# Latent attention on one core: head-by-head scaling on GpSimd, and more of the block transfers issued there

## The reference

```python
q = einsum('bld,dhk->blhk', xn, Wq)          # 16 heads of 64
latent = einsum('bld,dc->blc', xn, Wkv_down) # 64 numbers per token
k = einsum('blc,chk->blhk', latent, Wk_up)
v = einsum('blc,chk->blhk', latent, Wv_up)
attn = softmax(where(causal, q @ k / sqrt(64), -inf))   # per head, over keys
s = einsum('bqhd,hdo->bqo', attn @ v, Wout)
```

## Time and profile before

| | us |
|---|---|
| median of three runs | 2358.87 |
| profiled execution, time | 2362.68 |
| its span, first to last instruction | 2360.9 |
| PE busy | 2083.6 (88%) |
| DVE busy | 1713.2 (73%) |
| POOL busy | 1501.1 (64%) |
| ACT busy | 1314.0 (56%) |
| 1400 to 2360 us: PE, DVE, POOL busy | 834.56, 732.20, 724.99 |
| the same stretch, granted clock, DMA share | 0.92, 0.70 |

### The profile page before, as it was taken

One profiled execution on the slowest core, in us unless ns is written; L12 is line 12 of the kernel. 1 busy time (PEld: TensorE's weight loads), 2 busy tenths in 40 slices (PEclk: granted clock), 3 DMA queues, 4 the chain that ended last, 5 costly groups with the idle time before them and its releaser, 6 DMA issues. The chain is left out here.

```text
span 2360.9 us, 45085 instructions
## 1 busy us (share of the span) xinstructions
PE 2083.6 (88%) x15232; PEld 1619.0 (69%) x15232; DVE 1713.2 (73%) x3132; ACT 1314.0 (56%) x3178; POOL 1501.1 (64%) x1337
## 2 busy tenths in 40 slices
PE   6579999999899899999998678889998988898885
PEld 4467777777777777777777566667676767676764
DVE  5587776777767887777674277787788778877783
ACT  3346666766576567666674264545554565455541
POOL 2475666656655666566663147786778777877874
PEclk8789999999999999999999889999998999999988
DMA  8343333333333433333322127676767676767675
GB/s 278 96 104 78 91 93 90 81 90 86 91 79 98 112 88 77 83 88 92 85 66 72 73 75 167 183 180 160 185 179 184 164 188 172 186 167 182 167 178 142
DMA packets 190049, 298.19 MB, mean 126 GB/s; under 512 B 52264, under 2 KB 97660, under 8 KB 188796
## 3 DMA queue, kind: packets, MB, share of 16 engines
q1 hardware_dynamic: 172924, 257.53, 42.8%
q10 hardware_dynamic: 12288, 24.13, 4.2%
q0 software_dynamic: 4608, 13.64, 2.3%
HBM read 56.04 MB, written 20.97 MB: 33 GB/s over the span
## 5 line engine op out<-in xcount | busy, mean ns | idle before, releaser
L1750 PE MATMUL ps<-g_turned,g_latV 128*64 128x256 f32 (+1 forms) x1984 | 306.9, 456 | 47.9 <-issue 22.9
L2032 POOL TENSOR_TENSOR g_pt<-g_pt,g_rl 128x1024 f32<-128x1024 f32 (+2 forms) x112 | 293.8, 2628 | 62.5 <-DVE g_rl L1966 58.3
L854 ACT ACTIVATE l_pp<-ps,l_mx 128x256 f32<-128x256 f32 (+1 forms) x512 | 228.8, 464 | 162.9 <-DVE l_mx L991 162.9
L2032 POOL TENSOR_TENSOR g_pp<-g_pp,g_rl 128x768 f32<-128x768 f32 (+3 forms) x112 | 239.2, 2142 | 74.2 <-DVE g_rl L1966 73.4
L1130 POOL TENSOR_TENSOR l_pp<-l_pp,l_rl 128x1024 f32<-128x1024 f32 (+1 forms) x128 | 229.7, 1795 | 83.5 <-DVE l_rl L999 83.5
L1854 ACT ACTIVATE g_pp<-ps,g_mx 128x128 f32<-128x128 f32 (+3 forms) x256 | 173.5, 688 | 180.1 <-DVE g_mx L1948 78.0
L1854 ACT ACTIVATE g_pt<-ps,g_mx 128x256 f32<-128x256 f32 (+3 forms) x256 | 201.3, 798 | 122.4 <-DVE g_mx L1948 73.1
L1750 PEld LDWEIGHTS ps<-g_turned,g_latV 128*64 128x64 f32 x1984 | 149.5, 149 | 144.5 <-issue 88.9
L1147 POOL TENSOR_TENSOR l_act_lo<-l_u,l_act_hi 114x512 fp32r<-114x512 f32 x96 | 125.6, 1308 | 163.9 <-ACT l_act_hi L904 163.7
L1980 DVE STREAM_TRANSPOSE g_bt<-g_pt 128x1024 f32<-128x1024 f32 (+1 forms) x176 | 194.9, 1129 | 31.3 <-issue 12.6
L991 DVE CUSTOM_DVE_ANT_0 ps<-ps,l_mask 128x256 f32<-128x256 f32 (+1 forms) x512 | 188.4, 441 | 8.0 <-PE ps L703 8.0
(11 more groups left out here) (200 smaller groups left out, 6206.5 us busy)
## 6 DMA issues: line engine op xcount, KB each, us to landing
l_pt<-l_bt SPq DMA_DIRECT2D x1024, 64.0 KB, 2.0
g_turned<-g_bt SPq DMA_DIRECT2D x288, 128.0 KB, 3.4
g_turned<-g_bt SPq DMA_DIRECT2D x288, 96.0 KB, 2.5
g_turned<-g_bt SPq DMA_DIRECT2D x192, 112.0 KB, 3.0
g_turned<-g_bt SPq DMA_DIRECT2D x192, 80.0 KB, 2.4
l_tab<-turns SPq DMA_DIRECT2D x64, 128.0 KB, 2.1
g_turned<-g_bt ACTq DMA_DIRECT2D x64, 128.0 KB, 4.1
g_turned<-g_bt SPq DMA_DIRECT2D x96, 64.0 KB, 2.0
```

What stands on the lines that cost most here:

```text
L854: act.activation(PP[:, i % NP, at, 0:n], ps[:, bank + a, jj * 2 * P:jj * 2 * P + n], ACT.Exp, bias=mx[:, g % 2, h, at:at + 1], scale=-1.0, ...
L1750: last = pe.matmul(o, latV[:, b % 2, c, :], turned[:, :, a, c, :, :], start=(c == 0), stop=(c == t), skip_group_check=True)
L2032: pool.tensor_tensor(view, view, rl[:, u % 2, mine(k):mine(k) + n].unsqueeze(2).to_broadcast([P, n, keys(u)]), ALU.mult).then_inc(s["scale ...
```

## The change

Three things are changed at once.

First, for tiles 4 to 7 the scaling is done head by head. Each of the two heads of a step gets a TENSOR_SCALAR whose factor is one number per partition, in place of one TENSOR_TENSOR over both. `scaled` counts heads and no longer steps, so that the transpose of the first head waits for that head alone. Short tiles keep their instruction.

Second, the transfers are shared out anew:

| units | SP | ACT | POOL |
|---|---|---|---|
| short, before | 12 | 4 | 0 |
| short, now | 11 | 2 | 3 |
| long, before | 12 | 2 | 2 |
| long, now | 10 | 2 | 4 |

Third, the planner's numbers are others (COST, all of RANK, the cost of the two events), so the order on all engines is another one.

```diff
-    ASIDE = (((0, 0), (1, 1), (2, 2), (3, 3)),) * LONG + (((0, 0), (1, 1)),) * (NT - LONG)
-    BELOW = ((),) * LONG + (((2, 2), (3, 3)),) * (NT - LONG)
-    COST = (5.066, 3.78, 2.794, 2.559, 4.043, 4.94, 3.575, 3.892)
+    ASIDE = (((0, 0), (1, 1)),) * LONG + (((0, 0), (1, 1)),) * (NT - LONG)
+    BELOW = (((2, 2), (3, 3), (0, 1)),) * LONG + (((2, 2), (3, 3), (0, 1), (1, 2)),) * (NT - LONG)
+    COST = (4.133, 3.956, 2.412, 2.415, 6.582, 4.423, 1.923, 5.704)
...
-        "pool": {"split_x": -32.9, "scale": -8.81, "divide": 18.37, "move": -1.14},
-        "sp": {"xn": 13.3, "f": -27.73, "x": 55.61, "move": -13.19, "store": 61.01},
+        "pool": {"split_x": -63.04, "scale": -18.63, "divide": 15.72, "move": 0.58},
+        "sp": {"xn": -29.07, "f": 6.53, "x": 30.67, "move": -13.51, "store": 15.24},
...
-            return {"share": 0.12, "exp": 0.235 + 0.00084 * w, "scale": 0.06 + 0.00183 * w * heads}.get(
+            return {"share": 0.12, "exp": 0.235 + 0.00084 * w,
+                    "scale": 0.12 + 0.001 * w if self.long(n) else 0.06 + 0.00183 * w * heads}.get(
...
-            return {"act": 0.635 * aside, "pool": 1.0 * below, "sp": 0.635 * (16 - aside - below)}[engine]
+            return {"act": 0.65 * aside, "pool": 0.53 * below, "sp": 0.635 * (16 - aside - below)}[engine]
...
-                        dve.wait_ge(s["scaled"], first[u - 1])
+                        dve.wait_ge(s["scaled"], heads[first[u - 1]])
...
-                    dve.wait_ge(s["scaled"], k + 1)
+                    dve.wait_ge(s["scaled"], heads[k] + a + n)
...
-                def scale(k):
+                def scale(k, a):
 
                     u, p = pairs[k]
                     pool.wait_ge(s["rl"], k + 1)
-                    n = plan.wide(units[u][1])
+                    n, at = plan.wide(units[u][1]), mine(k, a)
+                    if plan.long(k):
+                        pool.tensor_scalar(probs(k, a), probs(k, a), rl[:, u % 2, at:at + 1], None, ALU.mult
+                                           ).then_inc(s["scaled"], 1)
+                        return
                     view = probs(k, 0, n).rearrange("p (a n) -> p a n", a=n)
                     pool.tensor_tensor(view, view, rl[:, u % 2, mine(k):mine(k) + n].unsqueeze(2).to_broadcast([P, n, keys(u)]),
-                                       ALU.mult).then_inc(s["scaled"], 1)
+                                       ALU.mult).then_inc(s["scaled"], n)
```

More of the change, by code:

```diff
@@ L1180 @@
     LONG = NT // 2
-    ASIDE = (((0, 0), (1, 1), (2, 2), (3, 3)),) * LONG + (((0, 0), (1, 1)),) * (NT - LONG)
-    BELOW = ((),) * LONG + (((2, 2), (3, 3)),) * (NT - LONG)
-    COST = (5.066, 3.78, 2.794, 2.559, 4.043, 4.94, 3.575, 3.892)
+    ASIDE = (((0, 0), (1, 1)),) * LONG + (((0, 0), (1, 1)),) * (NT - LONG)
+    BELOW = (((2, 2), (3, 3), (0, 1)),) * LONG + (((2, 2), (3, 3), (0, 1), (1, 2)),) * (NT - LONG)
+    COST = (4.133, 3.956, 2.412, 2.415, 6.582, 4.423, 1.923, 5.704)
     RANK = {
[L1185 to L1190, removed]
-        "pool": {"split_x": -32.9, "scale": -8.81, "divide": 18.37, "move": -1.14},
-        "sp": {"xn": 13.3, "f": -27.73, "x": 55.61, "move": -13.19, "store": 61.01},
+        "pe": {"latent": -46.39, "values": -18.27, "query": -40.4, "scores": -24.34, "weigh": 9.36, "wout": 40.96,
+              "back": 23.84},
+        "act": {"split_x": 36.71, "latent": -40.62, "values": -46.6, "query": -41.22, "exp": -15.61, "evacuate": -5.65,
+              "gate": -13.09, "move": -3.02},
+        "dve": {"latent": -25.14, "query": -44.88, "largest": 9.59, "share": 2.47, "blocks": 23.4, "gate": 12.45,
+              "back": 36.84},
+        "pool": {"split_x": -63.04, "scale": -18.63, "divide": 15.72, "move": 0.58},
+        "sp": {"xn": -29.07, "f": 6.53, "x": 30.67, "move": -13.51, "store": 15.24},
     }
@@ L1226, in __init__ @@
         events = {"scores": [e for k in range(K) for e in self.steps(k)], "share": [("share", k) for k in range(K)],
-                  "exp": [("exp", k, a) for k, a in heads], "scale": [("scale", k) for k in range(K)],
+                  "exp": [("exp", k, a) for k, a in heads], "scale": [("scale", k, a) for k, a in some],
                   "largest": [("largest", k, a) for k, a in apart], "blocks": [("blocks", k, a) for k, a in some],
@@ L1337, in needs @@
             elif kind == "share":
-                out += [("act", end(n))] + ([("pool", ("scale", last))] if lead else [])
+                out += [("act", end(n))] + ([("pool", tail("scale", last))] if lead else [])
             elif kind == "scale":
@@ L1341, in needs @@
             else:
-                out += [("pool", ("scale", n))]
+                out += [("pool", ("scale", n, event[2]))]
                 if lead and event[2] == 0:
@@ L2064, in _ @@
                     elif e[0] == "scale":
-                        scale(e[1])
+                        scale(e[1], e[2])
                     elif e[0] == "divide":
```

## The result

| | time | ratio to before, 95% interval |
|---|---|---|
| before | 2358.33 us | |
| changed | 2566.32 us | 1.0876 [1.084, 1.0913] |

The change makes the launch 208 us slower. I had forecast 2330, and 2368 as the upper end. The profiled execution has a span of 2563.1 us. First the page's chain of the changed kernel, then its windows (columns as in the earlier trace rows; the stage now runs from 1356 to 2560 us).

A forecast was written before the change was run, and what follows sets the result against it. SP's queue issuing block transfers, 23.6% of the chain, was taken as the bound, PE close behind. Terms -34 -6 +4 +1 = -35 us, cut by 6 to -29 for PE, gave 2330 us against the median; range 2298 to 2368.

The forecast's parts named there:

- The scaling: Long tiles on POOL: 256 one-head instructions priced like a CAST, 230 us in place of 379.5, 150 less.
- dear end: Long tiles' scaling on POOL if TENSOR_SCALAR runs as TENSOR_TENSOR does: 1.67 ns per element, 404 us, 25 more.
- Its worth: Cheaper scaling's effect on time: half of DVE's 11.8 us of waits for POOL credited, 6 us; ends 0 and 12.
- SP's issues: SP's queue: 160 fewer issues, 115 us, of which 29% on the path: 34 us gained; bounds 0 and 115.
- POOL's queue: 224 more issues on POOL at 520 ns, 116 us, queue 691 us in all; cost taken 4 us, bounds 0 and 23.
- the landing: Transfers issued from POOL land later than from SP (128 KB: 4.0 against 3.4 us); cost taken 1 us.
- rival B: PE and DVE take up SP's slack at once; time within 6 us either way, say 2355; chance 0.22.
- 20 as a sign of being wrong: Forecast wrong if DVE's waits for POOL's scaling or PE's for transfers grow by more than 20 us.
- The order: New ranks on all engines: taken as 0, with some 20 us possible either way.
- D: POOL becomes the late queue, with scaling at the dear end, from about 1.5 ns an element; 2374 us; chance 0.12.
- C: More than the sum: waits vanish on both sides, PE runs closer and its clock rises; 2306 to 2295; chance 0.14.
- over 1.3 us speaks for D: Sign on POOL: a one-head TENSOR_SCALAR was expected at 0.72 to 1.05 us; above 1.3 us favours D.

The follow-up runs named there:

- two_only: Kernel before, old order and shares, long tiles scaled per head by a two-operation TENSOR_SCALAR (multiply, add 0.0); 2350.69 us, ratio 0.9976.
- share_only: Kernel before with only the new shares of transfers on SP, ACT and POOL; order and scaling as before; 2345.07 us, ratio 0.9959.
- after_two: Changed kernel with each long-tile head scaled by a two-operation TENSOR_SCALAR (multiply, add 0.0) in place of one operation; 2360.75 us, ratio 1.0019.
- tt_step: Changed kernel, its order and shares, with long tiles scaled again by one TENSOR_TENSOR over both heads; 2417.97 us, ratio 1.0271.
- share_two: Kernel before in its own order, with the new shares and the per-head two-operation scaling of long tiles; 2360.94 us, ratio 0.9994.
- tt_head_planned: Changed kernel with per-head TENSOR_TENSOR scaling and the order planned anew with that instruction's measured price; 2430.59 us, ratio 1.0314.
- tt_head: Changed kernel, its order and shares, with each long-tile head scaled by a TENSOR_TENSOR (one number per partition spread); 2383.66 us, ratio 1.0136.
- ts_only: Kernel before with only the long tiles' scaling changed to one-operation TENSOR_SCALARs per head; order and shares kept; 2459.29 us, ratio 1.0447.
- share_head: Kernel before in its own order, with the new shares and long tiles scaled by a TENSOR_TENSOR per head; 2349.59 us, ratio 0.9976.

## Why the prediction was wrong

**The scaling: the step that failed.** "I take the end of the CAST, since it too has one tensor input": 230 us were forecast, 602 us measured. My dear end was 404 us, "that the operation runs as the TENSOR_TENSOR does", and I took it for a bound, though no row of before had a TENSOR_SCALAR wider than 16 elements. Those that it had, of 214 ns at 16 elements, multiply by -0.5 and add 1.5, so they are of the cheap form and couldn't have shown the dear one. The runs show 2.50 ns an element with one operation and 0.84 ns with two and a factor per partition, (1119 - 795) / 384. The cheap end was right for an instruction that isn't in the kernel. Exchanging the form in the changed kernel moves the time by 8.6% (1.0876 to 1.0019).

**Its worth.** With the cheap form and nothing else changed, the 6 us that I credited came out: two_only, 0.9976. With an interval of 1 to 10 us that is partly luck.

**SP's issues.** -34 us were forecast from SP's share of the chain; together with POOL's queue and the landing (+5) that makes -29. share_only measured -10 us. The 160 issues left SP, its waits for transposes rose from 70 to 110 us (I had said over 120), and its part of the chain fell by 172 us, five times what I had claimed. The mechanism is as predicted and its size is off: a share of one chain prices a removal only if the next way is much shorter. Here PE's was about as long, which was rival B. I had the hint, PE at 93 and 97% in the windows, and cut 6 us for it where the sum missed by 19. That PE took all 19 is argued from the chain and not shown.

**POOL's queue and landing.** Each issue took 511 ns (520 forecast). POOL's idle time in front of them was 36 us, not the 60 to 100 that I named, since a full queue waits less; with the cheap form (after_two) it is 80. A 128 KB transfer from POOL lands in 4.9 us in the changed kernel (4.1 in share_only), not 4.0, and PE's waits for transfers grew by 77 us, where I had named 20 as a sign of being wrong. In share_only both terms are hidden: they are part of its gain of 10 us.

**The order.** I took 0, with 20 us to each side. At a TENSOR_TENSOR's price it costs 73 us (tt_step beside share_only), and 6 us at the cheap one (after_two 1.0019 beside share_two 0.9994, the intervals overlap). So the term isn't a constant. Part of the way is seen: the new order puts the scaling on the way of DVE's transposes (99.6 us of waits in tt_step, 20.7 in after_two, 5.5 in share_only). But that isn't all of it. tt_head_planned has 6.3 us of work between `share` and transpose again and only 8.0 us of these waits, and it is slower than tt_head by 47 us. What the runs in a new order share is longer waits for landed transfers: DVE 31 to 33 us and PE 25 to 35 in tt_step, tt_head, tt_head_planned and after_two, beside 11 and 20 in share_only. Which wait makes the 73 us isn't shown.

With the one-operation form, the same exchange costs 8.6% with the new shares and order and 4.7% with the old ones (1.0447 against 0.9976). The traces have a simple account of that difference, which needs no order: the changed kernel's POOL has 1075 us of work in its stage and ts_only's has 966, 109 us more, and its span is 109 us longer (2563.1 against 2454.1). Nearly all of this work is the added issues, 178.4 us in place of 67.7. So once POOL is full, what is put on its queue seems to be paid in full, where in share_only the same issues cost nothing that could be seen. No run has the one-operation form with the new shares in the old order, so this is not shown apart from the order.

**The rivals.** D named what happened: POOL full, deciding from about 1.5 ns an element. It was given 0.12 and 2374 us, since I worked its time out from the dear end of a bound that wasn't one. D's own case, the scaling at a TENSOR_TENSOR's price with the new shares, was run as well: share_head in the order of before has POOL busy 869 of 994 us (87%) and loses nothing, 0.9976, and tt_head in the new order loses 32 us, 1.0136, where D said 15. So POOL at 87% of the stage wasn't late yet, and at 88 to 89% (ts_only and the changed kernel) it was. By D's own sum POOL passes 88% at 1.57 ns an element, not at 1.5. B was nearer than the forecast on SP's part: with the shares alone the time fell by 10 us, where B allowed 6 and my terms made 29. C, a clock that rises and brings time, wasn't seen. In the changed kernel the granted clock was 0.86 while PE was busy 77% of the stage; in after_two it was 0.95 from 1400 to 2320 us, where it was 0.93 before, and the time stood still. Of the signs that I named, "over 1.3 us speaks for D" was the one that decided.

**What stays open.** Why share_two gains nothing where its two parts each gain is not settled; the differences are of 0.2 to 0.4%, all its executions but the long one lie between 2345 and 2368 us, a wide spread beside these differences, and its interval overlaps that of share_only and that of two_only. Which of the new ranks costs the 73 us wasn't tried.

## What to carry to other kernels

A price for an instruction holds for its form, the number of its operations too, and a bound taken from other instructions isn't a safe one: where no row shows the very form at about this width, let the range reach beyond the dearest neighbour, or measure it by itself first, as one run with seven kinds of probe did here. A queue that leads the chain is worth its share only as far as the second longest way allows; look at the busiest engine in the windows before multiplying. And when a step is cheapened and moved in one go, try the new form in the old order first: here that run (ts_only) alone shows that the new form is the dear one, without the new order beside it.

## What the runs showed of the hardware

On an idle GpSimd, for 1024 fp32 elements of 128 partitions, each form run once: TENSOR_SCALAR with one operation 2.84 us (factor per partition), 2.89 (constant), 3.00 (addition); with two operations 1.05 (constants), 1.12 (one factor per partition), 1.20 (two, multiply and add), 1.35 (two, multiplied). A copy 1.04, TENSOR_TENSOR 1.89 whether its second input is spread or full. Working in place makes no difference at 1024 elements (2842 and 2842 ns; 1122 and 1124). At 256 and 512 elements the one-operation form took 0.15 us longer in place than out of place (1073 and 1713 ns against 927 and 1567). The neutral second operation, an addition of 0.0, makes the instruction 2.5 times as fast at 1024 elements and 1.9 times at 256 (927 and 482 ns).
